# Runs of four key tiles in the wide cross-attentions, and the additions of weights ordered one tile at a time

## The chip, the cores and the metric

The kernel runs on one core of one Trainium2 chip. The metric is the device time in microseconds (us) of one execution. TensorE is called PE here, VectorE DVE, ScalarE ACT, GpSimd POOL and SyncE SP, as in the profile.

## The reference

Four transformer layers are applied one after the other to x of shape (8, 256, 128): eight samples of 256 tokens. Each layer is a self-attention, a cross-attention over a context of 1601 tokens of width 96, and a feed-forward part. Layers 0 and 2 have wide heads (16 heads of 64), layers 1 and 3 narrow ones (16 heads of 8). What the change touches is the cross-attention of layers 0 and 2:

```python
sim = jnp.einsum('bihd,bjhd->bhij', q, k) * scale
attn = jax.nn.softmax(sim, axis=-1)
out = jnp.einsum('bhij,bjhd->bihd', attn, v).reshape(b, n, -1)
return out @ Wo + bo
```

Here i runs over 256 queries and j over 1601 keys.

## The kernel before

**Units.** The work is cut into units. A wide unit is one sample, one attention and one pair of heads (8 units for a sample), a narrow unit four heads (4 for a sample). The samples go in pairs: both samples of a pair go through one attention before the next begins, so that one round over all attentions is made four times. The attentions are numbered: 0 and 6 are wide self-attentions, 1 (with rotary positions) and 7 are wide cross-attentions, 3 and 9 narrow self-attentions, 4 and 10 narrow cross-attentions. There are 16 units in each visit of a wide cross-attention, 8 visits, so 128 such units.

**Within a unit.** The keys are cut into tiles of 128; a cross-attention has 13 (`kt`), the last of 65 rows. For each tile of a wide unit PE makes the scores (`make_scores`, L1562; four f16 matmuls of 256 columns), ACT takes the exponential into `probs` (`exps`, L1770), PE multiplies with the values into `o_acc` (`weigh_values`, L1587), and POOL adds the tile of `probs` to `weight_sum` (`add_weights`, L1292), for the denominator. `probs` has 8 buffers (`PROBS`, L26), `scores` 3, and the other results of PE go through a `ring` of 4 banks. Once the last tile is added, the job `sum` on PE sums `weight_sum` over the keys with a matrix of ones, DVE takes the reciprocal (`o_inv`), and POOL multiplies (`divide`, L1313). Further jobs of a unit are `op` (queries and keys, with rotation on DVE in attention 1), `max` (matmuls whose row maxima DVE takes), `shift` (the maximum put into the queries) and `val` (the values of the keys).

**Two shapes of matmul.** The value matmuls and the `sum` job write 64 of the 128 output partitions each, one head beside the other (32 in narrow units); all others use the whole array. `in_tiles` (L375) names the first sort. In the trace one tile of values of a wide unit is four f32 records, a pair of tiles eight, and a `sum` job four.

**Pairs.** Both the value matmuls and the additions go by pairs of tiles: `tiles(pair)`, `chunks_of(pair)` and `adds(pair)` (L92 to L101) say which tiles and which additions belong to a pair; a cross-attention has 7 pairs, the last of one tile. `weigh_values` and `add_weights` wait for the last exponential of the pair. An exponential that reuses a buffer of `probs` waits until the pair that read it is through on PE and added on POOL.

**The order.** No engine chooses at run time: each has one fixed list. `make_order` (L209) gives each piece a due time. The values of pair p are due at (p + 0.6) x time / 7 from the unit's start, with `time` 28 for attention 1 and 26 for attention 7; scores of a tile are due by the time of the tile three before it, counted from the first pair's due time (`place_scores`, L241); the `sum` job is due 3.5 after the last pair. `Plan.run` (L666) then goes through these with rough durations: each engine takes, of the pieces whose inputs are ready, the one due first. For PE, a piece that would change between the two shapes counts as due 1.0 (`STAY`, L28) later:

```python
if e == "PE" and in_tiles(what) != tiled:
    due = due[0] + STAY, due[1]
```

Of the kernel before, what the change touches and what calls it, by code (L numbers as in the profile page):

```python
# [33 lines left out]
class Attention:  # L34


    def __init__(self, sub, wide, cross, rope=False, src=None, time=0.0):
# [5 lines left out]
        self.pairs = -(-self.kt // 2)  # L43
# [48 lines left out]
    def tiles(self, pair):  # L92
        return range(2 * pair, min(2 * pair + 2, self.kt))

    def chunks_of(self, pair):

        return range(2 * pair * self.halves, min(2 * pair + 2, self.kt) * self.halves)

    def adds(self, pair):

        return 1 + 2 * pair - (pair == self.pairs - 1 and self.kt % 2)  # L101
# [107 lines left out]
def make_order():  # L209
# [54 lines left out]
    def place_jobs(un):  # L264
# [40 lines left out]
        for j, kind in enumerate(kinds):  # L305
            if kind == "sum":
                last = un.p == t.units - 1
                at = values_at[n, t.pairs - 1] + (2.0 if last else 3.5 if t.cross else t.time + 0.6)
# [7 lines left out]
            if kind == "val":  # L316
                if n >= 2:
                    at = max(at, values_at[n - 2, UNITS[n - 2].t.pairs - 1] + 0.0001)
                at = min(at, value - 0.0001 * (len(kinds) - j))
# [6 lines left out]
    for un in UNITS:  # L326
# [15 lines left out]
        ends[t.sub, un.u] = values_at[n, t.pairs - 1] + (4.5 if t.wide else 1.5)  # L342
# [37 lines left out]
class Plan:  # L380
# [4 lines left out]
    def __init__(self, static):  # L385
# [3 lines left out]
        for time, i, one in static:  # L389
            place = {"pre": self.pre, "job": self.job, "scores": self.scores, "values": self.values,  # L390
                     "close": self.close, "scale": self.scale, "copy": self.copy, "expand": self.expand,
# [7 lines left out]
    def chunk_parts(self, g):  # L399
        un, c = CHUNKS[g]  # L400
        pair = c // un.t.halves // 2
        out = [("PE", ("values", un.n, pair))]
        if un.t.wide:
            out.append(("POOL", ("values", un.n, pair)))
        return out

    def pre(self, due, one):
# [42 lines left out]
        elif kind in ("keys", "queries"):  # L450
            deps = [("DVE", here(of_kind(s, "hn" if s == 9 else "ln")[-1]))]
            if kind == "keys" and t.cross:
                deps = [] if u else [("ACT", here(m - 1))]
                if j == 0:
                    old = last_of(s - 3, u - u % 2 + 1)
                    deps.append(("PE", ("values", old.n, old.t.pairs - 1)))
# [68 lines left out]
    def wide_job(self, due, one, un, t, n, j, kind, i, k, pe):  # L525
# [31 lines left out]
        elif kind == "val":  # L557
            back = 2 if t.cross else VS_SLOTS
            deps = self.inputs(un) if i == 0 else []
            if at >= back:  # L560
                old = self.wide[at - back]
                deps.append(("PE", ("values", old.n, old.t.pairs - 1)))
# [7 lines left out]
        else:  # L570
            self.part("PE", "sum", due, one, 0.55, [("POOL", ("values", n, t.pairs - 1))], 0.2)
# [34 lines left out]
    def values(self, due, one):  # L606
        _, n, pair = one
        un = UNITS[n]
        t = un.t
        deps = [("ACT", ("scores", un.chunk + c)) for c in t.chunks_of(pair)]  # L610
        if pair == 0:
# [8 lines left out]
        tiles = len(t.tiles(pair))  # L620
        self.part("PE", "values", due, one, 0.43 * tiles, deps, 0.25)
        if t.wide:
            if pair == 0 and un.wide_at:
                old = self.wide[un.wide_at - 1]
                deps = [*deps[:t.chunks_of(0)[-1] + 1], ("PE", ("job", old.n, old.t.sum_job))]
            adds = t.adds(pair) - (t.adds(pair - 1) if pair else 0)
            self.part("POOL", "add", due, one, 1.3 * adds, deps)

    def close(self, due, one):
        n = one[1]  # L630
        un = UNITS[n]
        deps = [("PE", ("values", n, un.t.pairs - 1))]
# [167 lines left out]
def build(nc, a):  # L800
    with ExitStack() as ctx:
# [126 lines left out]
        av_done = per_unit("av_done", lambda un: un.t.pairs)  # L928
        weight_step = per_unit("weight_step", lambda un: un.t.adds(un.t.pairs - 1) if un.t.wide else 0)
# [293 lines left out]
        def _(pool):  # L1223
# [21 lines left out]
            def program():  # L1245
# [46 lines left out]
                def add_weights(un, pair):  # L1292

                    t, n = un.t, un.n
                    pool.wait_ge(exp_done.sem, exp_done.at(n, t.chunks_of(pair)[-1] + 1))
                    done = t.adds(pair - 1) if pair else 0
                    if pair == 0 and un.wide_at:

                        old = wide_before(un)
                        pool.wait_ge(*full(("job", old.n, old.t.sum_job)))  # L1300
                    for k in t.tiles(pair):
                        rows_ = t.rows(k)
                        total = weight_sum[0:rows_, :, :].rearrange("p h n -> p (h n)")
                        if k == 0:
                            continue
                        before = probs[0:rows_, un.chunk % PROBS, :] if k == 1 else total
                        if k > 1:
                            pool.wait_ge(weight_step.sem, weight_step.at(n, done))
                        pool.tensor_tensor(total, before, probs[0:rows_, (un.chunk + k) % PROBS, :], ALU.add)\  # L1309
                            .then_inc(weight_step.sem, 1)  # L1310
                        done += 1
# [33 lines left out]
        def _(pe):  # L1345
# [12 lines left out]
            def program():  # L1358
# [126 lines left out]
                def wide_job(one):  # L1485
# [22 lines left out]
                    if kind == "sum":  # L1508
                        pe.wait_ge(weight_step.sem, weight_step.at(n, t.adds(t.pairs - 1)))
# [77 lines left out]
                def weigh_values(n, pair):  # L1587
                    un = UNITS[n]
                    t = un.t
                    if pair == 0:  # L1590
# [11 lines left out]
                    pe.wait_ge(exp_done.sem, exp_done.at(n, t.chunks_of(pair)[-1] + 1))  # L1602
                    v = values_of(un)
                    for k in t.tiles(pair):
# [25 lines left out]
        def _(act):  # L1630
# [7 lines left out]
            def program():  # L1638
# [131 lines left out]
                def exps(g):  # L1770
# [534 lines left out]
```

## Time and profile before

| | |
|---|---|
| Median of 3 runs | 6563.81 us (6561.1 to 6564.27) |
| Profiled execution, its own time | 6570.67 us |
| Its span, first to last instruction | 6568.9 us |
| PE busy | 6072.1 us, 92% |
| DVE busy | 4851.4 us, 74% |
| ACT busy | 4175.0 us, 64% |
| POOL busy | 2747.1 us, 42% |
| Mean granted clock of PE | 0.967 |

The span leaves out 1.8 us of the profiled execution. The busy time of PE counts the modelled end of each pipelined matmul, so it says that PE had work, not that it ran at its peak. The share of an engine is a mean over stages of very different kind, so the stages have to be read one by one: attention 1 is first at work from 217.3 to 636 us, attention 7 first from 1024.5 to 1397 us.

### The profile page before, as it was taken

The page shows a single profiled execution, that of the slowest core. Times are in us where ns is not written, and L with a number is a line of the kernel's source. Part 1 is how long each engine was busy: PE and PEld are TensorE (multiplying, and loading weights), DVE is VectorE, ACT ScalarE, POOL GpSimd, SP SyncE. Part 2 cuts the span into 40 slices and gives each one's busy share as a digit, 9 for nine tenths or more (in the row PEclk, how much of TensorE's full clock was granted, in tenths as well). Part 3 has the DMA queues.
Part 4 walks back from the last instruction along what each step waited for, and adds up shares of the span by engine and source line. Part 5 has one row for each costly group of instructions (what it writes and reads, how often), then busy time and mean ns, then how long its engine had stood idle before and what let it go on. Part 6 is the DMA issues. An engine that isn't in the chain of part 4 may idle for free.

```text
span 6568.9 us, 122562 instructions
## 1 busy us (share of the span) xinstructions
PE 6072.1 (92%) x42376; PEld 3586.6 (55%) x42376; DVE 4851.4 (74%) x9782; ACT 4175.0 (64%) x9228; POOL 2747.1 (42%) x2358
## 2 busy tenths in 40 slices
PE   7999999989899998998989999899898999989988
PEld 5566456654556645664455654566445665456644
DVE  6887776657788777675878877667578886876656
ACT  4556676656655668665765666766575566776656
POOL 3466115751246612564025651266402655126630
PEclk8999999999999999998999999999898999999989
DMA  3111011100111101111011100111001111011100
GB/s 87 36 33 26 22 35 31 28 25 19 48 34 33 27 21 37 30 32 28 13 50 36 33 27 19 38 30 33 23 18 49 31 30 30 16 41 30 28 20 12
DMA packets 347662, 204.18 MB, mean 31 GB/s; under 512 B 165005, under 2 KB 319981, under 8 KB 346926
## 3 DMA queue, kind: packets, MB, share of 16 engines
q1 hardware_dynamic: 347054, 196.34, 11.8%
q8 instruction: 350, 5.73, 0.4%
q14 instruction: 258, 2.11, 0.1%
HBM read 105.18 MB, written 1.05 MB: 16 GB/s over the span
## 4 chain that ended last, share of the span: by engine, by line
PE 73%; DVE 10%; ACT 7%; issue 5%; POOL 4%; SPq 1%; DVEq 0%; DMA 0%; POOLq 0%; ACTq 0%
PE ring L1347 37%; PE o_acc L1347 18%; PE scores L1347 17%; DVE max_part L2097 3%; POOL weight_sum L1309 3%; ACT probs L1782 2%; ACT qop L1636 2%; DVE o_inv L2120 1%; POOL qm L1328 1%; DVE region L2059 1%; DVE qop L2056 1%; ACT qm L1636 1%; DVE ring L2073 1%; PE ring L1451 0%; DVE ring L2076 0%
## 5 line engine op out<-in xcount | busy, mean ns | idle before, releaser
L2097 DVE TENSOR_REDUCE max_part<-ring 128x1 f32<-128x400 f32 (+2 forms) x4608 | 2412.7, 577 | 567.4 <-PE ring L1347 543.8
L1782 ACT ACTIVATE probs<-scores 128x512 f32<-128x512 f32 (+1 forms) x3840 | 2105.9, 599 | 1051.5 <-PE scores L1347 961.8
L1309 POOL TENSOR_TENSOR weight_sum<-weight_sum,probs 128x512 f32<-128x512 f32 (+1 forms) x1408 | 1785.7, 1268 | 201.9 <-ACT probs L1782 66.8
L1347 PE MATMUL o_acc<-probs,region 128*32 128x256 f32 (+2 forms) x13312 | 1348.2, 388 | 11.3 <-ACT probs L1782 6.8
L1636 ACT ACTIVATE region<-ring 64x400 f16<-64x400 f32 (+4 forms) x1744 | 820.4, 480 | 480.6 <-PE ring L1347 291.9
L1309 POOL TENSOR_TENSOR weight_sum<-probs 128x512 f32<-128x512 f32 x256 | 325.4, 1271 | 1619.5 <-PE ring L1347 1194.3
L1347 PEld LDWEIGHTS o_acc<-probs,region 128*32 128x32 f32 (+2 forms) x13312 | 586.0, 122 | 547.0 <-issue 202.4
L1347 PE MATMUL scores<-qop,region 128*128 128x256 f16 (+1 forms) x3328 | 804.1, 274 | 11.3 <-ACT qop L1636 7.8
L1347 PE MATMUL scores<-qop,x_cop 128*128 128x256 f16 (+1 forms) x3328 | 800.1, 273 | 0.0
L1347 PE MATMUL ring<-nk,qm 128*128 128x400 f16 (+2 forms) x2560 | 709.5, 337 | 51.9 <-DVE max_part L2097 19.7
L1347 PE MATMUL scores<-qm,nk 128*128 128x512 f16 (+1 forms) x1920 | 657.3, 389 | 62.1 <-ACT probs L1782 32.0
L1636 ACT ACTIVATE qop<-ring 64x256 f16<-64x256 f32 (+1 forms) x1536 | 562.5, 375 | 177.0 <-PE ring L1347 86.7
L1328 POOL TENSOR_TENSOR qm<-nq,head_mask 128x1024 f16<-128x1024 f16 x128 | 242.1, 1894 | 1021.1 <-PE scores L1347 986.5
L2059 DVE TENSOR_TENSOR region<-ring,region 64x400 f16<-64x400 f32 (+1 forms) x1024 | 590.3, 576 | 71.2 <-ACT region L1636 52.2
L1347 PE MATMUL ring<-region,qop 128*128 128x400 f16 (+1 forms) x2048 | 598.5, 338 | 40.5 <-DVE region L2059 19.9
L2120 DVE RECIPROCAL o_inv<-ring 128x256 f32<-128x256 f32 x256 | 448.9, 1754 | 88.5 <-PE ring L1347 84.6
L1347 PEld LDWEIGHTS ring<-nk,qm 128*128 128x128 f16 x2560 | 232.9, 99 | 411.8 <-DVE max_part L2097 140.6
L1347 PEld LDWEIGHTS scores<-qop,region 128*128 128x128 f16 (+1 forms) x3328 | 327.6, 98 | 221.9 <-issue 106.7
L1347 PE MATMUL ring<-src_t,stage 96*128 96x400 f32 (+1 forms) x1024 | 425.2, 520 | 7.0 <-ACT qop L1636 4.2
L2056 DVE TENSOR_TENSOR qop<-ring,qop 64x256 f16<-64x256 f32 x512 | 214.3, 418 | 271.8 <-ACT qop L1636 268.0
L1347 PEld LDWEIGHTS scores<-qop,x_cop 128*128 128x128 f16 (+1 forms) x3328 | 329.0, 99 | 107.7 <-issue 31.0
L1347 PEld LDWEIGHTS ring<-region,qop 128*128 128x128 f16 x2048 | 188.7, 97 | 310.2 <-issue 208.3
(170 smaller groups left out, 7265.9 us busy)
## 6 DMA issues: line engine op xcount, KB each, us to landing
x_cop<-region SPq DMA_DIRECT2D x256, 200.1 KB, 3.1
stage<-in_wide SPq DMA_DIRECT2D x512, 64.0 KB, 2.0
nk<-region SPq DMA_DIRECT2D x192, 100.1 KB, 2.2
stage<-in_wide SPq DMA_DIRECT2D x128, 128.0 KB, 2.6
v_stage<-in_wide SPq DMA_DIRECT2D x256, 64.0 KB, 1.9
wo_stage<-in_wide SPq DMA_DIRECT2D x32, 512.0 KB, 4.0
cop_few<-kop_few SPq DMA_DIRECT2D x256, 32.0 KB, 1.9
ff_w<-in_ff_w SPq DMA_DIRECT2D x24, 256.0 KB, 3.4
```

The costliest lines, as they stand in the source:

```text
L1309: pool.tensor_tensor(total, before, probs[0:rows_, (un.chunk + k) % PROBS, :], ALU.add)\
L1328: pool.tensor_tensor(qm[:, un.narrow_at % QM_SLOTS, :, :], nq[:, z, :].unsqueeze(1).broadcast_to([P, 4, N]), head_mask[:, :].unsqueeze(2). ...
L1347: return pe.matmul(out, lhs, rhs, start=start, stop=stop, skip_group_check=True)
L1636: return act.activation(out, src, ACT.Identity, **kw)
L1782: act.activation(to, src, ACT.Exp, scale=t.scale).then_inc(exp_done.sem, 1)
L2056: last = dve.tensor_tensor(qop[part, z, 2 + h, :], v[part, 0:N], qop[part, z, h, :], ALU.subtract)
L2059: last = dve.tensor_tensor(kop[other, h, a0:a0 + w], v[part, 0:w], kop[part, h, a0:a0 + w], ALU.subtract)
L2073: dve.tensor_tensor(v, v, rope_sin[:, a0:a0 + w], ALU.mult).then_inc(rope_step.sem, 1)
L2097: dve.tensor_reduce(dst, src, AX.X, ALU.max).then_inc(*release(one))
L2120: dve.reciprocal(o_inv[:, un.wide_at % 2, :], ring[:, bank(one), 0:N]).then_inc(*release(one))
```

## The change

In the wide cross-attentions a run of value matmuls takes four tiles, so that a unit has 4 runs (4, 4, 4 and 1 tiles) in place of 7 pairs. All other attentions keep runs of two. The number of matmuls, of exponentials and of additions, and their shapes, stay the same.

The due times follow: the values of run r are due at (r + 0.6) x time / 4, and with them all that is counted from the first or last run. A run waits for the exponential of its last tile; an exponential that reuses a buffer waits for the whole run that read it.

The additions on POOL are no longer tied to the values: each is a piece of its own ("add"), placed and waited for tile by tile, due at (k + 0.5) x time / kt. An exponential that reuses a buffer waits for the addition of that tile alone. This holds for all wide attentions.

```
-        self.pairs = -(-self.kt // 2)
+        self.run = 4 if wide and cross else 2
+        self.runs = -(-self.kt // self.run)
...
-    def adds(self, pair):
-
-        return 1 + 2 * pair - (pair == self.pairs - 1 and self.kt % 2)
+    def adds(self, tile):
+
+        return max(tile, 1)
...
-        for pair in range(t.pairs):
-            values_at[n, pair] = clock + (pair + 0.6) * t.time / t.pairs
-            put(values_at[n, pair], "values", n, pair)
-        put(values_at[n, t.pairs - 1] + 0.0005, "close", n)
+        for run in range(t.runs):
+            values_at[n, run] = clock + (run + 0.6) * t.time / t.runs
+            put(values_at[n, run], "values", n, run)
+        for k in range(1, t.kt) if t.wide else ():
+            put(clock + (k + 0.5) * t.time / t.kt, "add", n, k)
+        put(values_at[n, t.runs - 1] + 0.0005, "close", n)
...
-            self.part("PE", "sum", due, one, 0.55, [("POOL", ("values", n, t.pairs - 1))], 0.2)
+            self.part("PE", "sum", due, one, 0.55, [("POOL", ("add", n, t.kt - 1))], 0.2)
...
+    def add(self, due, one):
+        _, n, k = one
+        un = UNITS[n]
+        deps = [("ACT", ("scores", un.chunk + k))]
+        if k == 1 and un.wide_at:
+            old = self.wide[un.wide_at - 1]
+            deps.append(("PE", ("job", old.n, old.t.sum_job)))
+        self.part("POOL", "add", due, one, 1.28, deps)
...
-                def add_weights(un, pair):
+                def add_weights(un, k):
...
+                    pool.wait_ge(exp_done.sem, exp_done.at(n, k + 1))
...
-                def weigh_values(n, pair):
+                def weigh_values(n, run):
...
-                    pe.wait_ge(exp_done.sem, exp_done.at(n, t.chunks_of(pair)[-1] + 1))
+                    pe.wait_ge(exp_done.sem, exp_done.at(n, t.chunks_of(run)[-1] + 1))
...
-                        pair = co // old.t.halves // 2
-                        act.wait_ge(av_done.sem, av_done.at(old.n, pair + 1))
+                        act.wait_ge(av_done.sem, av_done.at(old.n, co // old.t.halves // old.t.run + 1))
                         if old.t.wide:
-                            act.wait_ge(weight_step.sem, weight_step.at(old.n, old.t.adds(pair)))
+                            act.wait_ge(weight_step.sem, weight_step.at(old.n, old.t.adds(co)))
```

## Rows read from the trace of the kernel before

**Rows 1.** The page: span, busy times, and two of its costliest groups.

```profile
span 6568.9 us, 122562 instructions
...
PE 6072.1 (92%) x42376; PEld 3586.6 (55%) x42376; DVE 4851.4 (74%) x9782; ACT 4175.0 (64%) x9228; POOL 2747.1 (42%) x2358
...
L2097 DVE TENSOR_REDUCE max_part<-ring 128x1 f32<-128x400 f32 (+2 forms) x4608 | 2412.7, 577 | 567.4 <-PE ring L1347 543.8
...
L1347 PE MATMUL o_acc<-probs,region 128*32 128x256 f32 (+2 forms) x13312 | 1348.2, 388 | 11.3 <-ACT probs L1782 6.8
```

**Rows 2.** The page: the chain that ended last, by engine.

```profile
PE 73%; DVE 10%; ACT 7%; issue 5%; POOL 4%; SPq 1%; DVEq 0%; DMA 0%; POOLq 0%; ACTq 0%
```

**Rows 3.** Busy time in three stretches: attentions 1, 7 and 4.

```profile
217.30:636.00 418.70, 414.55 (x2804) 263.72 (x2804) 357.40 (x692) 250.82 (x517) 265.40 (x221) 1.00 0.13 32
...
1024.50:1397.00 372.50, 368.88 (x2644) 235.31 (x2643) 250.45 (x457) 240.12 (x506) 263.05 (x217) 1.00 0.12 30
...
726.40:900.20 173.80, 165.17 (x1399) 77.12 (x1399) 126.50 (x269) 135.70 (x295) 14.82 (x14) 1.00 0.07 16
```

**Rows 4.** Timeline of PE, one unit's period in attention 1.

```profile
358.14 0.65 PE L1347 MATMUL ring<-weight_sum,ones 128*64 128x256 f32 x4
358.62 1.03 PE L1347 MATMUL o_acc<-probs,region 128*64 128x256 f32 x8
359.59 0.34 PE L1347 MATMUL ring<-region,qop 128*128 128x401 f16 x1
...
362.80 1.08 PE L1347 MATMUL o_acc<-probs,region 128*64 128x256 f32 x8
363.81 1.61 PE L1347 MATMUL ring<-src_t,stage 96*128 96x400 f32 x4
...
366.65 0.33 PE L1347 MATMUL ring<-region,qop 128*128 128x400 f16 x1
366.91 1.95 PE L1347 MATMUL o_acc<-probs,region 128*64 128x256 f32 x16
368.79 1.16 PE L1347 MATMUL ring<-v_stage,src_t 96*128 96x128 f32 x8
...
372.23 0.68 PE L1347 MATMUL ring<-region,qop 128*128 128x400 f16 x3
...
384.01 0.65 PE L1347 MATMUL ring<-weight_sum,ones 128*64 128x256 f32 x4
```

**Rows 5.** Timeline of PE, one unit's period in attention 7.

```profile
1140.24 0.65 PE L1347 MATMUL o_acc<-probs,region 65*64 65x256 f32 x4
...
1144.09 1.08 PE L1347 MATMUL o_acc<-probs,region 128*64 128x256 f32 x8
1145.00 0.60 PE L1347 MATMUL ring<-weight_sum,ones 128*64 128x256 f32 x4
...
1159.69 0.65 PE L1347 MATMUL o_acc<-probs,region 128*64 128x256 f32 x4
```

**Rows 6.** Timeline at the end of a visit of attention 1.

```profile
625.47 1.09 ACT L1782 ACTIVATE probs<-scores 128x512 f32<-128x512 f32 x2 [1.02 <-PE scores L1347]
...
625.80 1.08 PE L1347 MATMUL o_acc<-probs,region 128*64 128x256 f32 x8
...
627.79 1.08 PE L1347 MATMUL o_acc<-probs,region 128*64 128x256 f32 x8
```

**Rows 7.** Waits within 217.3 to 636 us (total us, times, longest).

```profile
POOL weight_sum L1309 <- PE ring L1347: 140.8, 14, 35.9
...
ACT probs L1782 <- POOL weight_sum L1309: 17.4, 6, 2.9
```

**Rows 8.** Timeline of POOL: additions back to back.

```profile
338.13 12.30 POOL L1309 TENSOR_TENSOR weight_sum<-weight_sum,probs 128x512 f32<-128x512 f32 x9
```

**Rows 9.** Attention 4: its value matmuls in 726.4 to 900.2 us, and one wait for an exponential.

```profile
L1347 PE MATMUL o_acc<-probs,region 128*32 128x256 f32 x768 | 51.5, 385 | 1.1 <-ACT probs L1782 0.6
...
786.97 0.41 PE L1347 MATMUL scores<-qm,nk 128*65 128x512 f16 x1 [0.26 <-ACT probs L1782]
```

More of the change, by code:

```diff
@@ L307, in place_jobs @@
                 last = un.p == t.units - 1
-                at = values_at[n, t.pairs - 1] + (2.0 if last else 3.5 if t.cross else t.time + 0.6)
+                at = values_at[n, t.runs - 1] + (2.0 if last else 3.5 if t.cross else t.time + 0.6)
                 put(at, "job", n, j)
@@ L341, in make_order @@
         place_jobs(un)
-        ends[t.sub, un.u] = values_at[n, t.pairs - 1] + (4.5 if t.wide else 1.5)
+        ends[t.sub, un.u] = values_at[n, t.runs - 1] + (4.5 if t.wide else 1.5)
     for u in (B - 2, B - 1):
@@ L400, in chunk_parts @@
         un, c = CHUNKS[g]
-        pair = c // un.t.halves // 2
-        out = [("PE", ("values", un.n, pair))]
+        out = [("PE", ("values", un.n, c // un.t.halves // un.t.run))]
         if un.t.wide:
-            out.append(("POOL", ("values", un.n, pair)))
+            out.append(("POOL", ("add", un.n, un.t.adds(c))))
         return out
@@ L606, in values @@
     def values(self, due, one):
-        _, n, pair = one
+        _, n, run = one
         un = UNITS[n]
         t = un.t
-        deps = [("ACT", ("scores", un.chunk + c)) for c in t.chunks_of(pair)]
-        if pair == 0:
+        deps = [("ACT", ("scores", un.chunk + c)) for c in t.chunks_of(run)]
+        if run == 0:
             if t.wide:
@@ L619, in values @@
                 deps.append(("ACT", ("close", n - 1)))
-        tiles = len(t.tiles(pair))
+        tiles = len(t.tiles(run))
         self.part("PE", "values", due, one, 0.43 * tiles, deps, 0.25)
[L622 to L627, printed above, removed]
+    def add(self, due, one):
[6 more added lines that the diff above has]
+        self.part("POOL", "add", due, one, 1.28, deps)
     def close(self, due, one):
@@ L631, in close @@
         un = UNITS[n]
-        deps = [("PE", ("values", n, un.t.pairs - 1))]
+        deps = [("PE", ("values", n, un.t.runs - 1))]
         if un.p == 0 and n:
@@ L1290, in pre @@
                             .then_inc(ones_set.sem, 1)
-                def add_weights(un, pair):
+                def add_weights(un, k):
                     t, n = un.t, un.n
[L1295 to L1311, printed above, removed]
+                    pool.wait_ge(exp_done.sem, exp_done.at(n, k + 1))
+                    rows_ = t.rows(k)
+                    total = weight_sum[0:rows_, :, :].rearrange("p h n -> p (h n)")
+                    if k > 1:
+                        before = total
+                        pool.wait_ge(weight_step.sem, weight_step.at(n, t.adds(k - 1)))
+                    else:
+                        before = probs[0:rows_, un.chunk % PROBS, :]
+                        if un.wide_at:
+                            old = wide_before(un)
+                            pool.wait_ge(*full(("job", old.n, old.t.sum_job)))
+                    pool.tensor_tensor(total, before, probs[0:rows_, (un.chunk + k) % PROBS, :], ALU.add)\
+                        .then_inc(weight_step.sem, 1)
                 def divide(un):
```

28 lines of the change are left out of this document (14 added, 14 removed).

## The prediction

> **What bounds the kernel now.** I read the page first. PE is busy 92% of the span, DVE 74%, ACT 64%, POOL 42% [rows 1], and the chain that ended last runs on PE for 73% of its length [rows 2]. These are means over unlike stages, so the busy times by stretch come next. In the first visit of attention 1 PE is busy 414.55 of 418.70 us, in that of attention 7 368.88 of 372.50, both at the full clock (1.00, so 2.4 GHz) [rows 3]. There PE has no room: it is idle for 1%, and whatever is taken from PE's list is taken from the time. DVE is at 85% in attention 1 (357.40 of 418.70) and 67% in attention 7, ACT at 60% and 64%, POOL at 63% and 71% [rows 3]. The eight visits make up about 4 x (418.7 + 372.5) = 3165 us, 48% of the span. The change edits these stages.
>
> A busy PE isn't a PE at its peak, so I looked at PE's timeline for what the change could take away, since it takes no matmul away. The reader is to compare starts, as the ends are modelled. A run of two value tiles holds PE from 362.80 to 363.81: 1.01 us. In the same unit two pairs happen to stand side by side, as 16 records: 366.91 to 368.79, 1.88 us [rows 4]. So two more tiles cost 0.87, a tile is 0.43 to 0.44, and a run pays about 0.14 to 0.15 on top of its tiles. A sum job with two tiles behind it takes 1.45 (358.14 to 359.59), three times 0.43 and again 0.15 [rows 4]. The way in costs too: matmuls of 400 f16 columns follow each other by 0.17 (three records last 0.68, one 0.34; half of the difference), but the first value matmul starts 0.26 after one (366.65, 366.91) [rows 4]. That is 0.09 more. Every change to the half-width shape and back costs PE 0.24 us however many tiles lie between.
>
> The Trainium skill has a cause for this: TensorEngine Tiling (Array Packing), Key Properties, says that changing the tiling mode, not just the tile, drains the engine. The trace agrees that a change costs, 0.24 us for both ways. TensorE: Matmul & The Clock Gate, in its step on the drain, gives about 128 cycles to a drain; at 2.4 GHz two of them would be an estimated 0.11 us, and the sum below would be 28 us in place of 61. The measured rows decide.
>
> **What the change removes.** It lowers the number of such visits to the half-width shape. It is not three for each unit, because some neighbours are joined already. In attention 1's steady state the period from one sum job to the next is 25.87 us (358.14 to 384.01) and holds six of them: the sum with pair 0, pair 1, pair 2, pairs 3 and 4 as one, pair 5, pair 6; the first, third, fourth and the next period's first are shown [rows 4]. In attention 7's there are seven in a period of some 23 us, the sum joined to pair 0 and the other six apart (first, second and last shown) [rows 5]. After the change a unit has four runs and a sum: five visits if the sum stands alone, four if it is joined to a run. Joining depends on the due times. Before, the sum is due at 26.4 + 3.5 = 29.9 (in attention 1's units of time) and the next pair 0 at 30.4, within the 1.0 that the planner grants, and the rows show them joined. After, the sum is due at 25.2 + 3.5 = 28.7 and the next run 0 at 28 + 4.2 = 32.2, 3.5 apart; it will be joined only where PE's list is late there. Run 3 is due 3.5 before the sum, no nearer. So:
>
> - none joined: 64 units x 1 + 64 units x 2 = 192 visits less, x 0.24 = 46 us
> - all joined: 64 x 2 + 64 x 3 = 320 less, x 0.24 = 77 us
> - I take half, 256 less: 61 us. PE is rarely exactly on the due times, and both ends stay in the range.
>
> **What it adds: later runs.** A run waits for the exponential of its fourth tile. Before, a pair was due 2.8 to 4.0 units after the scores it needed; now run 1 is due at 11.2 and its last scores at 12.8, run 2 at 18.2 and 21.4. The planner therefore puts these runs where it believes the exponential just done, with no slack, and what ACT is late by then falls on PE. Three runs in each of 128 units wait so, 384. All other PE work is queued behind a waiting run, ring jobs first, and DVE after them. Lower bound: nothing. The narrow cross-attentions' due times are just as tight (pair p due at 1.8 + 3.0p, its last scores at 1.8 + 3.2p), and in attention 4 PE was idle before 768 value records for 1.1 us in all [rows 9]. Upper bound: 0.26 us a run, the wait for an exponential shown at 786.97 [rows 9], 384 x 0.26 = 100 us. I take 0.01 a run, 4 us, by the row of the same kind of matmul.
>
> **Ends of the visits.** Where a visit ends, PE has only scores and values left: pairs follow each other at 1.99 us (625.80, 627.79) with two exponentials (1.09) between them [rows 6]. A first run of four needs two more exponentials: up to 1.09 us at each of 8 ends, 9 us; the lower bound is nothing, if preludes fill it. I take 7.
>
> **Longer stretches without ring jobs.** A run of four blocks PE's other work for 1.88 us, a pair for 1.01. DVE's row maxima take 0.577 each [rows 1], and four full banks give it 2.3 us of work, so it doesn't run dry; attention 1 has such a run in each period already [rows 4]. Nothing, then; if the banks are less than full, a DVE at 85% still has 15% to catch up.
>
> **Buffers of weights.** A run of four frees four of eight buffers at once. ACT can fill the other four meanwhile, and scores can be three more ahead. A run comes every 6 to 8 us and four exponentials take 2.2 (twice the 1.09 of two [rows 6]). Nothing.
>
> **Additions.** The same twelve per unit. Nine take 12.30 us back to back, 1.37 each [rows 8], so 16.4 of a period of 23 to 26. POOL mostly waits for PE's sum job (140.8 us in the visit) [rows 7], which now is due 1.2 earlier. The more waits POOL executes are covered by this idle time; without it a late addition would hold up an exponential. ACT's waits for additions, 17.4 us [rows 7], can shrink, but ACT isn't the bound: no gain counted. In self-attentions the one addition is due slightly later and the values are where they were: nothing, by POOL's idle time. No DMA is added. The weight and copy queue of SP keeps its triggers, some of them shifted by up to 1.8 units with the first run's due time; SP's loads are two units ahead.
>
> **The sum.** -61 + 4 + 7 = -50 us. The profiled execution would be 6570.7 - 50 = 6520.7; it stands 6.9 above the median, so I predict 6563.8 - 50 = 6514 us. Clock, span's remainder and stages outside the wide cross-attentions stay as they are.
>
> **Rivals.**
>
> 1. *Only part of a visit's price comes back.* If the 0.15 on the way out were the latency of the last values and still paid elsewhere, only the way in would count: 256 x 0.09 = 23 us, 6541. Against it: the 16-record run in the same unit really is 0.14 shorter than two of 8 [rows 4].
> 2. *The waits eat the gain.* From 0.13 us a run (50 / 384) nothing is left: 6564. For it: the due times leave no slack. Against: rows 9, and an ACT at 60 to 64%.
> 3. *Slower: PE starves as in the narrow stages.* In attention 4, with its tight due times, PE is idle 8.6 of 173.8 us, 5% in place of 1% [rows 3]. Were the wide cross-attentions to go to 5%, through scores held up by buffers that are freed by fours, the loss would be 4% of 3165 = 127 us against 61: 6630. It decides from 2% more idle. Against it: ACT is busy 135.70 of 173.80 there, 78% [rows 3], as a narrow unit has two exponentials for each tile of keys.
> 4. *The new list is differently good.* Every due time of these stages moves, and a greedy order can turn out some 0.3% better or worse (20 us) without a cause that these rows show. This is in the range, not a case of its own.
>
> **How the numbers follow.** Forecast (a gain of 30 to 85 us) 0.70; rival 1 0.10; rival 2, or a gain and a loss that cancel, 0.09; rival 3 in any size beyond 0.2% 0.11. A difference under 0.2%, 13 us, is about what a measurement of this kernel can't tell from none. Faster by more: 0.70 + 0.10 = 0.80; within: 0.09; slower: 0.11. Range: the low end is all sums joined without losses, 77 us, and a somewhat better list, 6482. The high end reaches through rival 1 to the edge of rival 2, 6552. The likeliest case's own range is 6482 to 6534.
>
> **What would show it.** Right: in attention 1's stretch value runs of 16 records three times a unit, 1.88 us each; PE's period down from 25.9 to 25.5 or less, in attention 7 from 23.0 to 22.5 or less; PE's busy time down with the span; idle time before value matmuls still some tens of us at most. The joined sums can be counted: rows of a sum job followed at once by value records. Wrong: long "idle before" ended by ACT's exponentials at the value runs (rival 2), idle time at scores (rival 3), a run of 16 longer than 1.9 us, or more PE busy time at the same number of matmuls.

## Result and the profile after

The changed kernel takes 6615.7 us (median of 4 runs, 6615.1 to 6618.3) against 6564.0 us before: a ratio of 1.008, 95% interval 1.0063 to 1.0097. It is slower by 52 us. The prediction was 6514 us, faster, with a range up to 6552. It came out the other way.

The page of the changed kernel, the lines that answer to [rows 1] and [rows 2], and two groups more (the last two numbers of a group: its busy time and mean ns, then the idle time before it and what ended most of it):

```profile
span 6616.6 us, 123210 instructions
...
PE 6024.8 (91%) x42376; PEld 3630.8 (55%) x42376; DVE 4845.8 (73%) x9782; ACT 4152.6 (63%) x9228; POOL 2749.6 (42%) x2358
...
PE 13%; ACT 2%; DVE 2%; issue 1%; POOL 1%; POOLq 0%; ACTq 0%; DVEq 0%
...
L2099 DVE TENSOR_REDUCE max_part<-ring 128x1 f32<-128x400 f32 (+2 forms) x4608 | 2408.9, 578 | 575.0 <-PE ring L1350 553.8
...
L1350 PE MATMUL o_acc<-probs,region 128*32 128x256 f32 (+2 forms) x13312 | 1275.6, 386 | 11.5 <-ACT probs L1784 6.5
...
L1350 PE MATMUL scores<-qop,region 128*128 128x256 f16 (+1 forms) x3328 | 799.9, 274 | 43.6 <-ACT qop L1639 37.5
...
L1350 PE MATMUL ring<-region,qop 128*128 128x400 f16 (+1 forms) x2048 | 582.4, 338 | 81.0 <-DVE region L2061 62.0
```

PE's busy time fell from 6072.1 to 6024.8 us, by 47, and the span grew by 48. So PE has less work and some 95 us more idle time. The value matmuls don't wait: 11.5 us, as before (11.3). The idle time stands before the scores, ended by ACT's queries (`qop`), and before the `max` matmuls, ended by DVE's rotated or added low part (`region`). The chain of waits adds up to 19% only; it breaks off early in this trace, so I don't use it.

Busy time in the first visits of attentions 1 and 7, which answer to the first two of [rows 3]:

```profile
219.70:642.40 422.70, 408.92 (x2785) 266.62 (x2785) 355.07 (x690) 246.25 (x516) 264.26 (x220) 1.00 0.12 32
1033.90:1409.80 375.90, 359.77 (x2623) 240.46 (x2622) 244.95 (x453) 236.47 (x501) 260.72 (x215) 1.00 0.11 30
```

PE is idle for 13.8 and 16.1 us, against 4.2 and 3.6 before. To compare all visits, the next table takes from PE's starts the length of a visit (first to last value record) and ("then") the time from its end to the first value record of the narrow cross-attention that comes next, 4 or 10, each as a mean over the four rounds. The steady period is that of one unit, from one 65-row tile to the next (in attention 1 before it varies from 25.79 to 26.03); "to half width" counts how often PE goes to the half-width shape in it.

| | attention 1 | then | attention 7 | then | steady period, to half width: 1 | 7 |
|---|---|---|---|---|---|---|
| before | 418.8 | 84.5 | 372.7 | 105.0 | 25.87, 6 | 23.01, 7 |
| after | 422.7 | 90.3 | 375.9 | 102.4 | 26.02, 5 | 23.48, 5 |

The loss sits in attention 1 and what follows it: (422.7 + 90.3) - (418.8 + 84.5) = 9.7 us, four times 39. Attention 7 with what follows it is level (+0.6 a round), though its steady period is 0.47 longer.

Over the whole trace PE goes to the half-width shape 1340 times after the change and 1572 times before: 232 ways less (a way is what the prediction calls a visit to that shape), 25 in each visit of attention 1 and 33 in each of attention 7.

**Attention 7, one unit's seam.** PE, then ACT, then DVE, in the changed kernel's timeline:

```profile
1124.23 0.65 PE L1350 MATMUL o_acc<-probs,region 65*64 65x256 f32 x4
...
1143.33 1.95 PE L1350 MATMUL o_acc<-probs,region 128*64 128x256 f32 x16
1145.21 0.30 PE L1350 MATMUL ring<-ident_half,pair_cols 128*65 128x128 f16 x2
1145.35 0.65 PE L1350 MATMUL ring<-h_t,stage 128*128 128x256 f32 x2
...
1147.72 0.65 PE L1350 MATMUL o_acc<-probs,region 65*64 65x256 f32 x4
...
1150.61 0.33 PE L1350 MATMUL ring<-region,qop 128*128 128x401 f16 x1
1151.93 0.33 PE L1350 MATMUL ring<-region,qop 128*128 128x401 f16 x1 [0.98 <-DVE region L2061]
```

```profile
1143.17 0.21 ACT L1639 ACTIVATE pair_cols<-max_of 128x4 f16<-128x4 f32 x1
...
1145.55 2.20 ACT L1639 ACTIVATE qop<-ring 1x256 f16<-1x256 f32 x6 [1.51 <-PE ring L1350]
1147.77 1.02 ACT L1639 ACTIVATE region<-ring 64x401 f16<-64x401 f32 x2
...
1149.57 2.05 ACT L1639 ACTIVATE region<-ring 64x400 f16<-64x400 f32 x4
```

```profile
1147.78 0.86 DVE L2058 TENSOR_TENSOR qop<-ring,qop 64x256 f16<-64x256 f32 x2 [4.64 <-ACT qop L1639]
...
1150.61 1.17 DVE L2061 TENSOR_TENSOR region<-ring,region 64x400 f16<-64x400 f32 x2 [0.63 <-ACT region L1639]
```

Read it from the top. The run of sixteen records holds PE for 1.88 us (1143.33 to 1145.21), just as predicted. Behind it stand the shift and the query job, and ACT had been idle for 1.51 us until they came. ACT then makes six copies (2.20), DVE had waited 4.64 for the queries, then for the keys, and its low part at 1150.61 is late. PE's next `max` matmul starts 1.32 us after the one before it, where two such matmuls otherwise follow each other by 0.17. It is one of 401 columns and the low part it waits for is one of 400, so it waits for a bank of the ring that DVE still reads, not for an operand. From 1124.23 to 1147.72 the period is 23.49 us; before it was 23.01 (the 65-row tile at 1140.24 of [rows 5] and its forerunner at 1117.23).

Before, the pair of tiles 10 and 11 stood behind the shift, at 1159.69 [rows 5], and no value matmul stood between the maxima and the shift:

```profile
1158.30 0.30 PE L1347 MATMUL ring<-ident_half,pair_cols 128*65 128x128 f16 x2
```

```profile
1158.05 0.20 ACT L1636 ACTIVATE pair_cols<-max_of 128x4 f16<-128x4 f32 x1
...
1159.07 2.19 ACT L1636 ACTIVATE qop<-ring 1x256 f16<-1x256 f32 x6
```

From the maxima (`pair_cols`) to the six copies it took 1.02 us before (1158.05 to 1159.07) and takes 2.38 now (1143.17 to 1145.55).

**Attention 1.** The same seam, with ACT's copies:

```profile
377.40 0.65 PE L1350 MATMUL o_acc<-probs,region 65*64 65x256 f32 x4
...
380.60 0.28 PE L1350 MATMUL ring<-ident_half,pair_cols 128*65 128x128 f16 x2
380.77 1.61 PE L1350 MATMUL ring<-src_t,stage 96*128 96x401 f32 x4
...
383.00 0.27 PE L1350 MATMUL scores<-qop,region 128*128 128x256 f16 x1 [0.61 <-ACT qop L1639]
...
403.42 0.65 PE L1350 MATMUL o_acc<-probs,region 65*64 65x256 f32 x4
```

```profile
380.66 2.20 ACT L1639 ACTIVATE qop<-ring 64x256 f16<-64x256 f32 x6
```

The first scores need ACT's six copies, done at 382.86. Between the shift and these scores PE has only the four `src_t` records to do. Before, a pair of values stood there too:

```profile
375.87 0.28 PE L1347 MATMUL ring<-ident_half,pair_cols 128*65 128x128 f16 x2
376.07 1.08 PE L1347 MATMUL o_acc<-probs,region 128*64 128x256 f32 x8
377.09 1.61 PE L1347 MATMUL ring<-src_t,stage 96*128 96x401 f32 x4
```

In the changed kernel that pair belongs to the run of tiles 8 to 11, which stands ahead of the shift. The pair had been the cover for the copies: from the start of the `src_t` records to the first scores it was 1.45 us (377.09 to 378.54), now it is 2.23 (380.77 to 383.00).

### The profile page after: what moved, and what is told of

Its sections match the earlier page's. It is cut to its first block and busy times, and to the rows that moved or that the text cites. A ratio compares the mean times of both kernels' runs of the same rounds, so it can differ in the third digit from the quotient of the medians.

```text
span 6616.6 us, 123210 instructions
## 1 busy us (share of the span) xinstructions
PE 6024.8 (91%) x42376; PEld 3630.8 (55%) x42376; DVE 4845.8 (73%) x9782; ACT 4152.6 (63%) x9228; POOL 2749.6 (42%) x2358
## 5 line engine op out<-in xcount | busy, mean ns | idle before, releaser
L1784 ACT ACTIVATE probs<-scores 128x512 f32<-128x512 f32 (+1 forms) x3840 | 2072.6, 598 | 722.7 <-PE scores L1350 693.3
L1350 PE MATMUL o_acc<-probs,region 128*32 128x256 f32 (+2 forms) x13312 | 1275.6, 386 | 11.5 <-ACT probs L1784 6.5
L1350 PEld LDWEIGHTS o_acc<-probs,region 128*32 128x32 f32 (+2 forms) x13312 | 614.2, 123 | 509.9 <-issue 134.4
L1350 PE MATMUL ring<-region,qop 128*128 128x400 f16 (+1 forms) x2048 | 582.4, 338 | 81.0 <-DVE region L2061 62.0
```

Source lines behind the costliest of these rows:

```text
L1350: return pe.matmul(out, lhs, rhs, start=start, stop=stop, skip_group_check=True)
L1784: act.activation(to, src, ACT.Exp, scale=t.scale).then_inc(exp_done.sem, 1)
```

## Experiments

Each kernel was timed beside the kernel before, on the same chip; times are medians. Ratios are against before, with their 95% interval. The first pair splits the change in two.

**Additions alone.** The changed kernel with runs of two everywhere.

```
-        self.run = 4 if wide and cross else 2
+        self.run = 2
```

> The additions are placed tile by tile as in the changed kernel, the values stay in pairs. Theory A (the loss comes from where PE's list puts the runs of four at the seam between two units: the first scores and the maxima now stand where nothing covers the chain in front of them): the additions have no part in it, 6564 us, within 0.2% of before. Theory B (a run of four is itself at fault, wherever it stands, since it waits for four exponentials, frees buffers by fours and shuts out the ring jobs): also 6564. Theory C (the additions, separate and due at other times, cost the time): near the changed kernel, 6600 to 6616.

Measured: 6563.0 against 6562.3 us, 0.9999 (0.9990 to 1.0008). The additions alone change nothing.

**Runs alone.** The kernel before with pairs of four tiles in the wide cross-attentions and the additions still tied to them.

```
-        self.pairs = -(-self.kt // 2)
+        self.run = 4 if wide and cross else 2
+        self.pairs = -(-self.kt // self.run)
...
-        return range(2 * pair, min(2 * pair + 2, self.kt))
+        return range(self.run * pair, min(self.run * (pair + 1), self.kt))
```

> Runs of four, but the additions stay tied to the runs (a run's additions are one piece, waited for by the run's last exponential). A and B: as slow as the changed kernel, 6605 to 6630. C: fast, about 6564 less the 46 us of the visits saved, 6518.

Measured: 6595.9 us, 1.0047 (1.0035 to 1.0060), below the 6605 of A and B and far above the 6518 of C. The steady periods are those of the changed kernel (26.02 and 23.48) and so are the visits (422.4 and 375.3), but the 20 us to 6615.7 are missing. The time after attention 1's visit is 84.5 here and 90.3 in the changed kernel: four times 5.8 is 23 us. The other stretches of the two profiles differ both ways and about cancel. So the additions do cost something, but only together with runs of four.

**Joined in place.** The lists of the kernel before, with each even pair of the wide cross-attentions taken out of PE's list and done with the odd one.

```
+            if one[2] % 2 == 0 and one[2] < t.pairs - 1:
+                continue
+            one = (*one[:2], one[2] // 2)
```

> The lists of the kernel before, with one edit: in the wide cross-attentions each even pair of value tiles is moved down to the odd pair behind it, so that runs of 4, 4, 4 and 1 tiles stand where pairs 1, 3, 5 and 6 stood; all else in the order of before. Five visits to the half-width shape a unit, as many as the changed kernel. A: the order is what costs, so the price of a visit comes back, 192 x 0.24 = 46 us less some idle time: 6515 to 6535. B: a run of four loses wherever it stands: 6580 to 6620.

Measured: 6628.0 us, 1.0103 (1.0088 to 1.0119): the slowest but one, where a gain was expected. Nothing is moved here but the even pairs (and the exponentials that reuse a buffer wait for a whole run), and still attention 1's visit takes 426.1 us and attention 7's 382.3. PE now waits in the middle of a unit, where the even pair had stood; the timeline of attention 1:

```profile
384.85 1.95 PE L1364 MATMUL o_acc<-probs,region 128*64 128x256 f32 x16
...
390.20 0.33 PE L1364 MATMUL ring<-region,qop 128*128 128x400 f16 x1 [0.47 <-DVE region L2076]
391.68 1.95 PE L1364 MATMUL o_acc<-probs,region 128*64 128x256 f32 x16
```

My theory in its simple form (the moves are free, only new due times are bad) fell with this. This kernel was not tried with more buffers, so how much of its loss is the wait of exponentials for whole runs isn't separated.

**Single tile first.** Runs of 1, 4, 4 and 4 tiles, each due by its last tile.

```
+        sizes = [1, 4, 4, 4] if wide and cross else [min(2, self.kt - k) for k in range(0, self.kt, 2)]
...
+            values_at[n, run] = clock + ((run + 0.6) * t.time / t.runs if not (t.wide and t.cross) else (t.cuts[run + 1] / 2 - 1 + 0.4) * t.time / 7)
```

> The changed kernel with runs of 1, 4, 4 and 4 tiles in place of 4, 4, 4 and 1, each due by its last tile as pairs were, so that a run of four is the last of its unit and can stand between the next unit's shift and its first scores. A: PE's idle time at the seam shrinks by most of its 0.7 us (attention 1) and 1.0 us (attention 7) a unit, and the visits' gain shows: 6500 to 6545. B: as many runs of four, as slow: 6600 to 6620.

Measured: 6510.8 us, 0.9926 (0.9913 to 0.9938). The same sizes of run in another order and with other due times (two edits that weren't tried apart) win 105 us over the changed kernel. PE goes to the half-width shape four times a unit: the single tile is joined to the sum job. The gain is in attention 7 (visit 366.1, then 96.7), while attention 1 is as slow as after the change (424.1, then 90.0).

**Split again.** The changed kernel's lists, each run of four cut in two by the piece that follows it.

```
+        if held and t is None:
+            out += [one, held]
...
+            out.append((*one, 0))
+            held = (*one, 1)
```

> The changed kernel's lists, with one edit on PE: each run of four value tiles is cut in two, and the piece that followed it stands between the halves, which makes three more visits to the half-width shape a unit and keeps ACT's waits for whole runs. If a visit costs PE 0.24 us here too: at most 384 x 0.24 = 92 us on top of the changed kernel, 6690 to 6708. If a long run does its harm by keeping ring jobs out for 1.9 us, the earlier ring piece gives some of it back: 6640 to 6680. If the visit's price were only a matter of how the records look: 6616.

Measured: 6697.1 us against 6563.0, 1.0206 (1.0192 to 1.0220). That is 81.4 us over the changed kernel. A steady unit has 3 more ways to half width, but where the piece that follows a run is a sum job no way is added: the trace has 1704 in place of 1340, 364 more and not 384. So 81.4 / 364 = 0.22 us each; the steady periods (26.79 and 24.13) give 0.26 and 0.22. The predicted price of 0.24 holds.

**Shift first.** In attention 1, ACT's two copies of the shift go ahead of the four of the queries where they stand side by side.

```
+            if s.sub == t.sub == 1 and s.jobs[a[2]][:2] == ("op", 0) and t.jobs[b[2]][0] == "shift":
+                out[i - 1:i + 1] = b, a
```

> The changed kernel, with one edit on ACT: in attention 1 the two copies of a unit's shift come before the four copies of the next unit's queries, where the two stand side by side (52 of 64 units). Theory A' (PE's idle 0.59 us before the first scores of each unit of attention 1 is a wait for the shift copies, which nothing covers since the value pair that stood there is gone): the copies are done 1.5 us sooner, the wait goes, 52 x 0.6 to 0.75 = 31 to 39 us less, 6577 to 6585. Rival (the period is set by another chain, DVE's, and the idle time only moves): 6605 to 6616.

Measured: 6609.3 us, 1.0075 (1.0063 to 1.0088). The waits of PE in the first visit of attention 1, the changed kernel and then this one (total us, times, longest):

```profile
PE scores L1350 <- ACT qop L1639: 8.7, 14, 0.8
```

```profile
PE ring L1364 <- DVE raw L2087: 1.9, 11, 0.2
PE ring L1364 <- DVE qop L2072: 1.3, 3, 0.8
...
PE scores L1364 <- ACT qop L1653: 0.7, 1, 0.7
```

The wait at the scores is gone, 8 us a visit, so it was a wait for the copies of the shift. But the period is 26.07 in place of 26.02 and the visit 424.1 in place of 422.7, as smaller waits at DVE take its place: the rival's case. The 6 us to the changed kernel are no gain that can be told from none, as the intervals of the two ratios overlap widely.

**Seam of attention 7 opened.** The second half of the third run is put behind the shift and the first query job, in 48 units.

```
+            if t.sub == 7 and one[2] == 2 and len(kinds) == 2 and kinds[0] and kinds[0][0] == "shift" and kinds[1] == ("op", 0):
+                out.append((*one, 0))
+                held, left = (*one, 1), 2
```

> The changed kernel, with one edit on PE: in attention 7, where run 2 of a unit stands right before the next unit's shift and first query job, its second half is moved behind those two (48 of 64 units). Theory A' (PE's idle 0.74 us a unit of attention 7 at the maxima comes from the query job held up behind the run of four, which leaves ACT and DVE late): the idle time and 0.16 us hidden in the record before it go, one visit of 0.24 is added, 48 x 0.66 = 32 us less, 6584. Rival (the run's place is not the cause): the added visit alone, 48 x 0.24 = 12 us more, 6628.

Measured: 6605.4 us, 1.0068 (1.0055 to 1.0080), 10 us less than the changed kernel; here too the intervals overlap (1.0063 to 1.0097), and it is far from the 32 us of theory A'. PE's waits for DVE's low part, from 1100 to 1350 us, the changed kernel and this one:

```profile
PE ring L1350 <- DVE region L2061: 7.9, 8, 1.0
```

```profile
PE ring L1376 <- DVE region L2089: 4.7, 8, 0.6
```

0.40 us of each wait is gone, so the late shift and queries are part of its cause; the extra way to half width (0.24) takes most of it back, and the period falls by 0.05 only.

**Single tile first in attention 7 only.** 1, 4, 4, 4 in attention 7, pairs in attention 1.

```
+        sizes = {1: [2, 2, 2, 2, 2, 2, 1], 7: [1, 4, 4, 4]}.get(sub) or [min(2, self.kt - k) for k in range(0, self.kt, 2)]
```

> Runs of 1, 4, 4 and 4 tiles, due by their last tile, in attention 7 alone; attention 1 keeps its pairs; additions tile by tile. With both changed so, attention 7's period fell by 0.55 us a unit and attention 1's by 0.15. If the two add up: 6510.8 plus 64 x 0.15 = 10 us, 6520. If DVE at 85% makes runs of four no gain in attention 1 once its ends are counted: as fast as with both or faster, 6500 to 6510.

Measured: 6476.1 us against 6563.0, 0.9875 (0.9860 to 0.9891). This is the fastest kernel of the study, 87 us better than before, and faster than either case of mine. Here is its PE around two single tiles, with the shift ahead of the first run shown:

```profile
1141.60 0.30 PE L1352 MATMUL ring<-ident_half,pair_cols 128*65 128x128 f16 x2
...
1145.21 1.95 PE L1352 MATMUL o_acc<-probs,region 128*64 128x256 f32 x16
...
1150.38 0.65 PE L1352 MATMUL o_acc<-probs,region 128*64 128x256 f32 x4
1150.87 0.60 PE L1352 MATMUL ring<-weight_sum,ones 128*64 128x256 f32 x4
1151.40 0.34 PE L1352 MATMUL ring<-region,qop 128*128 128x400 f16 x1
...
1172.44 0.65 PE L1352 MATMUL o_acc<-probs,region 128*64 128x256 f32 x4
```

The period is 22.06 us (1150.38 to 1172.44), 0.95 less than before. Three ways to half width at 0.24 make 0.72 of it. The last run of four stands behind the shift here, not ahead of it. Attention 7 and what follows it take 365.8 + 96.5 = 462.3 in place of 477.7: 15.4 a round, as 16 units of 0.95 (15.2) would have it. The visit is counted from its first value record, which comes sooner with a single tile first: the stretch from attention 4's first value record to it is 291.8 us in place of 296.6. With that the gain is 20.2 a round, 81 us in four.

**Runs of the change in attention 7 only.** 4, 4, 4, 1 in attention 7, pairs in attention 1.

```
+        sizes = {1: [2, 2, 2, 2, 2, 2, 1], 7: [4, 4, 4, 1]}.get(sub) or [min(2, self.kt - k) for k in range(0, self.kt, 2)]
```

> Runs of 4, 4, 4 and 1 in attention 7 alone, pairs in attention 1, additions tile by tile. In the changed kernel's steady state a unit of attention 7 takes 23.48 us against 23.01 before (0.47 more, x 64 = 30 us) and one of attention 1 26.02 against about 25.9 (0.13 more, x 64 = 8 us). If the two attentions' losses add up: 6590 to 6602. If most of the loss is attention 1's, with its DVE at 85%: 6560 to 6580.

Measured: 6567.4 us, 1.0004 (0.9995 to 1.0013), no difference from before. The changed kernel differs from this one in attention 1 alone, by 422.7 - 417.3 = 5.4 us in the visit and 90.3 - 83.9 = 6.4 behind it: four times 11.8 is 47 us, of the 48 between the two medians.

**Eleven buffers of weights.**

```
-RING, SLOTS, PROBS = 4, 3, 8
+RING, SLOTS, PROBS = 4, 3, 11
```

> The changed kernel with 11 buffers for the exponentials in place of 8; the lists of PE, DVE, POOL and SP stay the same and ACT's nearly so (some 20 pieces elsewhere). If runs of four lose by freeing buffers four at a time: part of the 52 us comes back, 6565 to 6600. If they lose by what stands uncovered at the seam between units: no change, 6608 to 6620.

Measured: 6621.2 against 6563.6 us, 1.0088 (1.0074 to 1.0101), with the same periods as the changed kernel. Buffers that come free by fours are not the cause in the changed kernel.

**ACT lighter, in the changed kernel and in the one before.** Two of the four copies of queries that ACT makes for a unit of attention 7 are left out, in each kernel.

```
-                            for to in (slice(0, 64), slice(64, 128)):
+                            for to in (slice(0, 64), slice(64, 128)) if t.sub != 7 else (part,):
```

> The changed kernel, leaving out two of the four copies that ACT makes of a unit's queries in attention 7 (so half of the query operands there are stale). They take 0.76 us and stand ahead of the copies of keys on ACT. If PE's wait of 1.15 us a unit of attention 7 (a maxima job for which no bank of the ring is free, since DVE's low part is late, since ACT's copies are late) is the chain that sets the period: it shortens by most of 0.76 us, 64 x 0.6 to 0.76 = 38 to 49 us, 6567 to 6578. If another chain sets it: 6605 to 6616.

> The same two copies left out of the kernel before, whose PE waits for nothing in attention 7: 6555 to 6567, no difference beyond 0.2%, by the first reading. If lighter ACT work helps any list: as much less as in the changed kernel.

Measured: changed kernel 6599.9 us (1.0053, 1.0040 to 1.0065), 16 less than without the edit and between my two cases; period 23.48 to 23.09. Kernel before 6537.1 us, 0.9962 (0.9950 to 0.9975), 26 less; period 23.01 to 22.67, where I expected no change. The gap between the two kernels did not close by the lighter ACT (63 us in place of 52), so the first result is no part of the 52 found. The second result is the one that speaks against my prediction's first step: in a stretch where PE counts as 99% busy, two copies less on ACT gave back 0.34 us a unit. Busy time from 1100 to 1350 us, in this order: before, before with the lighter ACT, changed, single tile first in attention 7 only:

```profile
1100.00:1350.00 250.00, 248.32 (x1762) 158.60 (x1760) 174.50 (x320) 164.59 (x345) 176.04 (x144) 1.00 0.12 31
```

```profile
1100.00:1350.00 250.00, 249.77 (x1783) 161.02 (x1781) 173.88 (x319) 160.24 (x332) 178.81 (x146) 1.00 0.11 29
```

```profile
1100.00:1350.00 250.00, 239.51 (x1717) 159.22 (x1716) 166.30 (x311) 162.29 (x344) 170.85 (x139) 1.00 0.11 29
```

```profile
1100.00:1350.00 250.00, 247.53 (x1801) 168.51 (x1800) 177.87 (x328) 169.25 (x361) 176.84 (x145) 0.99 0.13 32
```

Look at PE's busy time and its count of matmuls. Before and with the lighter ACT, PE is full (248.32 and 249.77 of 250), yet the second gets through 1783 matmuls, 21 more. Before, the starts show the gap: from the last score to the next `max` matmul 0.28 us a unit more than such records need, and from `max` to scores 0.23 more, hidden under ends that are modelled (a score's record is 0.27 long where the next may start after 0.11). Here is one such place before, the last score, the `max` matmul 0.38 us after it, and the next score 0.38 after that:

```profile
1118.76 0.27 PE L1347 MATMUL scores<-qop,x_cop 128*128 128x256 f16 x1
1119.14 0.33 PE L1347 MATMUL ring<-region,qop 128*128 128x401 f16 x1
1119.52 0.28 PE L1347 MATMUL scores<-qop,region 128*128 128x256 f16 x1
```

With the lighter ACT both distances are at their least in all places of the unit (0.11 and 0.17 to 0.18). The Trainium skill says the same of such records: Perfetto Trace Analysis, Tensor Engine Instruction (MATMUL, LD_WEIGHTS), calls their reported end an estimate; this pair of runs agrees.

The visits of all kernels that differ from before and after, as in the first table:

| | attention 1 | then | attention 7 | then |
|---|---|---|---|---|
| additions alone | 417.3 | 84.1 | 374.2 | 105.2 |
| runs alone | 422.4 | 84.5 | 375.3 | 100.2 |
| joined in place | 426.1 | 84.1 | 382.3 | 105.1 |
| single tile first | 424.1 | 90.0 | 366.1 | 96.7 |
| single tile first in 7 only | 417.3 | 84.3 | 365.8 | 96.5 |
| runs of the change in 7 only | 417.3 | 83.9 | 375.9 | 101.7 |

## Why the prediction was wrong, point by point

**Price of a change of shape: right.** 0.24 us predicted, 0.22 to 0.26 measured by cutting the runs again. A run of sixteen takes 1.88 us. The estimate from the Trainium skill, TensorE: Matmul & The Clock Gate, step on the drain (0.11 us), is half of what was measured; its statement in TensorEngine Tiling (Array Packing), Key Properties, that a change of mode drains the engine, agrees with these runs in that a change costs; that the cost is a drain no run here shows.

**Number of ways to the half-width shape: near, for another reason.** I took 256 less, as the middle between sums alone and sums joined to a run. The trace has 232 less, and hardly a sum is joined: a steady unit has five ways, the sum alone. What I had wrong is the count before. I took the six ways of attention 1's steady unit for all 16 units of a visit, but several of them have seven, so that a visit loses 25 and not 16; that this makes up for most of the joined sums I had hoped for is luck. At 0.24 us, 232 ways are 56 us. In the first two visits PE's busy time fell by 5.6 and 9.1 us, which times four is 59. Over the whole span it fell by 47 only, as it grew by 13 us in the four stretches behind attention 1. This term alone, 56 for 61, would have made 6519.

**Waits for exponentials, buffers, additions by themselves: right.** Idle time before value matmuls is 11.5 us (11.3 before), which refutes rival 2; eleven buffers give nothing back; the additions alone change nothing.

**The step that failed: "whatever is taken from PE's list is taken from the time".** It is wrong in two ways. First, PE was not without room in attention 7: a lighter ACT alone made that stretch faster, so part of PE's "busy" time was waiting under modelled ends, 0.51 us a unit. The prediction had said that the ends are modelled and then read the busy share as if they weren't. Second, and worth more, taking a pair out of its place takes away the cover of whatever runs beside it on other engines. I costed "Longer stretches without ring jobs" at nothing by counting how long four full banks feed DVE. I looked at DVE's maxima, and the chain that came up short was another: shift and queries on PE, copies on ACT, rotation or low part on DVE, then the scores or a bank of the ring for PE. In a steady unit of attention 7 two ways less save 2 x 0.24 = 0.48 us, and the period is 0.47 longer: 0.95 us of waits more than before. In attention 1 one way less saves 0.24, the new wait at the scores is 0.77 start to start, and some older waits shrink: 0.15 longer. "Joined in place" shows it most plainly: there only the even pairs moved, five ways were left in place of six or seven, and the kernel is slower still. In the sum of the prediction this is the term put at nothing, and over the visits it came to more than the gain: in the first two PE's idle time grew by 9.6 and 12.5 us, 88 in four rounds, against 59 of busy time saved.

**No single wait is the cause.** Removing the wait at attention 1's scores and opening the seam in attention 7 gave 6 and 10 us of 52, neither clear of the intervals, though in both the wait itself went or shrank. Other waits came up in its place, or an extra way to half width was paid. A kernel with runs of four and the old cover at every seam was not built, so the lost cover is shown as the source of these waits, and not by getting the time back. What did win was the other order and its due times, in which the single tile joins the sum and every other run is of four: no idle time shows at the seam of attention 7 (some waits under modelled ends are left, 0.3 us a unit), four ways, 22.06 us. How much of it is the order and how much the due times is open.

**Attention 1 gains nothing from runs of four.** In either order its visit is longer than with pairs (422.7 and 424.1 against 417.3), though it has fewer visits to half width. DVE is at 84% there (355.07 of 422.70) and ACT's copies and DVE's rotation both stand in front of the scores; which of them takes the gain was not separated.

**Ends of the visits: predicted +7 us, measured about +23 behind attention 1 (and 10 less behind attention 7).** This is the other half of the loss: the visits themselves are 7.1 us a round longer, 28 in all. The stretch behind attention 1, with the hand-off to the narrow self-attention, takes 90.3 in place of 84.5 us. Here is the second of four, before and after, and two of PE's waits at its start after the change:

```profile
2273.90:2355.40 81.50, 65.99 (x425) 35.33 (x423) 51.16 (x116) 46.44 (x115) 23.32 (x21) 0.92 0.13 33
```

```profile
2287.70:2376.70 89.00, 70.78 (x422) 39.05 (x420) 51.44 (x116) 45.90 (x114) 23.81 (x21) 0.85 0.12 30
```

```profile
2290.16 1.07 PE L1350 MATMUL o_acc<-probs,nv_few 128*32 128x256 f32 x16 [1.32 <-ACT probs L1784]
...
2292.88 1.12 PE L1350 MATMUL ring<-weight_sum,ones 128*64 128x256 f32 x4 [1.58 <-POOL weight_sum L1313]
```

Nearly the same number of matmuls (422 and 425) takes PE 70.78 us busy in place of 65.99, at a mean granted clock of 0.85 in place of 0.92. Over all four such stretches PE is busy for 288 us in place of 275, at 0.85 in place of 0.89. PE waits there for an exponential and for POOL's last addition (1.32 and 1.58 us). All seven kernels that have both runs of four in attention 1 and the additions tile by tile take 89.0 to 90.4 us here, all others 83.9 to 84.7. Why the two together do it was not tried, so the cause of this half stays open; that the waits bring the lower clock is only argued. Before, waits stand in the first 8 us of this stretch too, but none over 0.71 us.

**Rival 3 was nearest** (chance 0.11): PE's idle share in the visits rose from 1% to 3 to 4%, past its point of decision of 2% more. But its mechanism, scores held up by buffers freed in fours, is refuted by the eleven buffers, and what stood in its place is the lost cover. Rival 4, a list differently good, was kept as a spread of 20 us; the order of the list turned out to decide the sign: runs of four in both attentions gave 6511 us (single tile first), 6616 (the change) and 6628 (joined in place).

## What to carry to other kernels

When a piece of work is taken out of its place in a tight in-order list, price two things: what the piece costs, and what it covered. List the chains on other engines that ran beside it, with the work left between their start and their use. If a fixed cost per run is to be saved, try it per stage and in more than one place: for instance with the long run where a chain has just been started and the leftover tile where it joins other work of its shape, as the fastest kernel here has them.

A busy share of 99% from modelled ends doesn't show that an engine has no room. Compare starts with the least distance of such records, or make another engine lighter and see whether the stage moves.

## What the runs showed of the hardware

- A way to the half-width shape and back costs PE 0.22 to 0.26 us among full-array matmuls at the full clock (364 ways more, 81.4 us more).
- PE's records counted 248.32 of 250 us as busy in a stretch that still ran 1.5% faster (23.01 to 22.67 us a unit) when ACT had less to do.
- In the second stretch behind attention 1, 422 matmuls ran at a mean granted clock of 0.85, where 425 had run at 0.92 before, and took 4.8 us more of PE. It begins with PE waits of 1.3 and 1.6 us; that these bring the lower clock isn't shown.
